# A blend whose weights move to PSUM: four convolution layers on one core

## The reference

```
x = x + L0(_gn(x))   # 1x1 conv to 288, depthwise 3x3; 8x8 circular correlation of q and k by FFT,
                     # layer norm over channels, times v, 1x1 conv back to 48
x = x + L1(_gn(x))   # 1x1 conv to 288, a mask on the FFT of 8x8 patches, depthwise 3x3, gelu gate
x = x + L2(_gn(x))   # below
x = x + L3(_gn(x))   # 1x1 conv to 192, depthwise 3x3, gelu gate, 1x1 conv, FFT mask on 8x8 patches
```

```
integ = jnp.cumsum(jnp.cumsum(x, axis=-1), axis=-2)
...
A = _grid_sample_border_bilinear(integ, off_tl)      # Bt, Ct, D: the other three corners
return (A + D - Bt - Ct) / area
```

## Time and profile before

| | |
|---|---|
| median of three executions | 36,064.37 us (35,958.09 to 36,074.78) |
| profiled execution | 36,039.24 us |
| its span, first to last instruction | 36,037.1 us |
| PE, PEld, DVE, ACT, POOL busy | 84%, 49%, 54%, 20%, 27% |
| granted TensorE clock, mean | 0.869 |

### The profile page before, as it was taken

One profiled execution on the slowest core, in us unless ns is written; L12 is line 12 of the kernel. 1 busy time (PEld: TensorE's weight loads), 2 busy tenths in 40 slices (PEclk: granted clock), 3 DMA queues, 4 the chain that ended last, 5 costly groups with the idle time before them and its releaser, 6 DMA issues. The chain is left out here.

```text
span 36037.1 us, 386987 instructions
## 1 busy us (share of the span) xinstructions
PE 30354.0 (84%) x121076; PEld 17516.0 (49%) x121076; DVE 19585.9 (54%) x30068; ACT 7293.6 (20%) x13627; POOL 9842.8 (27%) x8820
## 2 busy tenths in 40 slices
PE   3999998877779999777789989677789988777899
PEld 2664446444444446444444455445444463444566
DVE  4336774444557774444457764444467744555433
ACT  1332221121222220111222210122122211111122
POOL 0000000266640000466620000666600002777300
PEclk9999996877779996877789978777799968888999
DMA  2110001433320003333310013333300014555332
GB/s 81 33 34 14 14 15 54 97 89 85 90 64 15 14 14 88 93 89 89 88 33 14 15 33 98 85 88 87 84 18 14 14 51 104 116 115 120 89 67 64
DMA packets 756453, 2226.31 MB, mean 62 GB/s; under 512 B 217460, under 2 KB 427444, under 8 KB 621240
## 3 DMA queue, kind: packets, MB, share of 16 engines
q1 hardware_dynamic: 314304, 1181.12, 14.0%
q0 software_dynamic: 441408, 1037.60, 11.2%
HBM read 1840.72 MB, written 385.13 MB: 62 GB/s over the span
## 5 line engine op out<-in xcount | busy, mean ns | idle before, releaser
L1486 POOL DMA_INDIRECT e_got<-table,e_idx x8192 | 9470.4, 1156 | 4874.5 <-issue 2568.6
L818 PE MATMUL b_p_conv<-b_z,b_diag 96*96 96x512 f32 (+1 forms) x11616 | 5289.4, 596 | 28.8 <-DVE b_acc L937 21.1
L937 DVE SCALAR_TENSOR_TENSOR b_acc<-b_z,b_dwc,b_acc 96x512 f32<-96x512 f32 (+1 forms) x6864 | 5144.6, 750 | 243.2
L488 PE MATMUL a_p_qk<-a_wst,a_stack 128*128 128x192 f32 x12288 | 2967.1, 369 | 1013.8 <-issue 958.1
L818 PEld LDWEIGHTS b_p_conv<-b_z,b_diag 96*96 96x96 f32 (+1 forms) x11616 | 1848.9, 167 | 2481.6 <-issue 2418.2
L780 POOL DMA_DIRECT2D planes<-b_out x132 | 68.0, 515 | 10895.6 <-DVE b_out L961 10895.6
L488 PEld LDWEIGHTS a_p_qk<-a_wst,a_stack 128*128 128x128 f32 x12288 | 2168.4, 206 | 1513.3 <-issue 1401.7
L280 PE MATMUL d_p<-d_xs,d_ws 128*96 128x512 f32 x9216 | 2575.5, 424 | 215.2 <-issue 187.1
L876 ACT ACTIVATE b_ys<-b_p_in 128x304 f32<-128x304 f32 x2112 | 892.9, 423 | 7948.0 <-PE b_p_in L827 7948.0
L840 PE MATMUL b_p_z<-const,b_ym 128*96 128x128 f32 (+1 forms) x12672 | 1880.2, 288 | 601.2 <-ACT b_z L882 518.1
L840 PEld LDWEIGHTS b_p_z<-const,b_ym 128*96 128x96 f32 (+1 forms) x12672 | 1713.3, 178 | 1097.1 <-ACT b_z L882 692.1
(11 more groups left out here) (261 smaller groups left out, 40035.1 us busy)
## 6 DMA issues: line engine op xcount, KB each, us to landing
e_got<-table,e_idx POOLq DMA_INDIRECT x8192
a_stack<-in_xp SPq DMA_DIRECT2D x256, 387.0 KB
c_stack<-planes SPq DMA_DIRECT2D x256, 387.0 KB
d_stack<-planes SPq DMA_DIRECT2D x256, 387.0 KB
table<-i_acc SPq DMA_DIRECT2D x256, 384.0 KB, 2.3
b_x<-planes SPq DMA_DIRECT2D x132, 395.1 KB
b_xr<-planes POOLq DMA_DIRECT2D x132, 395.1 KB, 4.7
planes<-b_out POOLq DMA_DIRECT2D x132, 395.1 KB, 4.1
```

The lines of the kernel that those rows point to most:

```text
L488: pe.matmul(dst_, st[:, row, dx + 128 * t:dx + 128 * t + 128], wst[:, dx, 0:2 * C2], start=(dx == 0), stop=False)
L818: mm = pe.matmul(p_conv[i % 2][0:M[g], :], diag[0:M[g], base + k, 0:M[g]], z[1 - par][g][0:M[g], QROWS * q + dy:QROWS * (q + 1) + dy, dx:d ...
L937: ins = dve.scalar_tensor_tensor(out=a, in0=z[1 - par][g][0:M[g], QROWS * q + dy:QROWS * (q + 1) + dy, dx:dx + W], scalar=dwc[0:M[g], g, k ...
L1486: pool.indirect_dma_start(out=self.got[k % 4][:, t, j * REC:(j + 1) * REC], out_offset=None, in_=self.flat, in_offset=bass.IndirectOffsetO ...
```

## The change

In the joint phases with layer 0, ScalarE copies the 64 weights of a unit from SBUF into columns 384 to 447 of the bank `p_f[0]` (`weigh`), one step before the blend, and VectorE's product reads them there and not in SBUF. A semaphore `wt_copied` tells VectorE that the copy is there; `weighted`, which the product now raises in place of the first count of `halved`, tells ScalarE that the columns may be written again, and TensorE that the transforms may write the bank. With layer 3 `bank` is None, and the product reads SBUF as before.

```diff
+        spare = p_f[0][:, 4 * C2:4 * C2 + 64]
...
-                def transforms(n, k):
+                def transforms(n, k, back2):
 
                     pe.wait_ge(qk_copied, 2 * (n + 1))
+                    if boxes and back2:
+
+                        pe.wait_ge(boxes.weighted, n - 2 - 4 * S + 1)
...
+                    if boxes and back:
+
+                        boxes.weigh(act, u if 1 <= k < 8 else u - 1, (k - 1) % 8, n - 1 - 4 * S, spare)
                     if back:
                         act.wait_ge(b_ready, n)
...
-                        boxes.blend(dve, u if 2 <= k < 8 else u - 1, (k - 2) % 8, n - 2 - 4 * S)
+                        boxes.blend(dve, u if 2 <= k < 8 else u - 1, (k - 2) % 8, n - 2 - 4 * S, spare)
...
-            credit(dve, self.halved, n=4)
+            credit(dve, self.weighted)
+            credit(dve, self.halved, n=3)
...
+    def weigh(self, act, u, k, n, bank):
+
+        i, q = k // 4, k % 4
+        if q == 0:
+            act.wait_ge(self.aux_loaded[i], (self.b * self.U + u + 1) * 32)
+        act.wait_ge(self.weighted, n)
+        act.activation(bank, self.wt[i][:, 64 * q:64 * q + 64], ACT.Copy).then_inc(self.wt_copied, 1)
+
+    def blend(self, dve, u, k, n, bank):
...
+        if bank is None:
+            bank = self.wt[i][:, 64 * q:64 * q + 64]
+        else:
+            dve.wait_ge(self.wt_copied, n + 1)
         flat = got[:].rearrange("p t (k c) -> p (t k) c", c=C)
-        dve.tensor_tensor(flat, flat, self.wt[i][:, 64 * q:64 * q + 64].unsqueeze(2).broadcast_to([128, 64, C]), ALU.mult).then_inc(self.halved, 1)
+        dve.tensor_tensor(flat, flat, bank.unsqueeze(2).broadcast_to([128, 64, C]), ALU.mult).then_inc(self.weighted, 1)
+        dve.wait_ge(self.weighted, n + 1)
         for j, half in enumerate((8 * C, 4 * C, 2 * C)):
-            dve.wait_ge(self.halved, n4 + j + 1)
+            if j:
+                dve.wait_ge(self.halved, n * 3 + j)
             dve.tensor_tensor(got[:, :, 0:half], got[:, :, 0:half], got[:, :, half:2 * half], ALU.add).then_inc(self.halved, 1)
...
-                            boxes.blend(dve, pair, place, at)
+                            boxes.blend(dve, pair, place, at, None)
```

More of the change, by code:

```diff
@@ L547, in step @@
                     if front:
-                        transforms(n, k)
+                        transforms(n, k, back2)
                     if back:
@@ L561, in _ @@
                     credit(act, qk_copied, qh_copied, upper_done, n=2)
+                if boxes:
+                    boxes.weigh_credit(act)
                 act.wait_ge(weights_loaded, 16 * NLOAD * (b + 1))
@@ L1420, in __init__ @@
         (self.halved, self.used, self.v_ready, self.y_ready, self.res_ready, self.stats_done, self.turn_sem, self.cleared,
-         aux0, aux1, x0, x1, s0, s1, idx0, idx1) = semaphores(env, "e", [
+         aux0, aux1, x0, x1, s0, s1, idx0, idx1, self.weighted, self.wt_copied) = semaphores(env, "e", [
              "halved", "used", "v_ready", "y_ready", "res_ready", "stats_done", "turn", "cleared",
-             "aux_loaded0", "aux_loaded1", "x_loaded0", "x_loaded1", "stored0", "stored1", "idx_loaded0", "idx_loaded1"])
+             "aux_loaded0", "aux_loaded1", "x_loaded0", "x_loaded1", "stored0", "stored1", "idx_loaded0", "idx_loaded1", "weighted", "wt_copied"])
         self.aux_loaded, self.x_loaded, self.stored, self.idx_loaded = [aux0, aux1], [x0, x1], [s0, s1], [idx0, idx1]
@@ L1498, in clear @@
         dve.wait_ge(self.cleared, 4 * (self.b + 1))
-    def blend(self, dve, u, k, n):
+    def weigh(self, act, u, k, n, bank):
[5 more added lines that the diff above has]
+    def blend(self, dve, u, k, n, bank):
         i, q = k // 4, k % 4
@@ L1506, in blend @@
             dve.wait_ge(self.aux_loaded[i], (self.b * self.U + u + 1) * 32)
+        if bank is None:
+            bank = self.wt[i][:, 64 * q:64 * q + 64]
+        else:
+            dve.wait_ge(self.wt_copied, n + 1)
         flat = got[:].rearrange("p t (k c) -> p (t k) c", c=C)
-        dve.tensor_tensor(flat, flat, self.wt[i][:, 64 * q:64 * q + 64].unsqueeze(2).broadcast_to([128, 64, C]), ALU.mult).then_inc(self.halved, 1)
+        dve.tensor_tensor(flat, flat, bank.unsqueeze(2).broadcast_to([128, 64, C]), ALU.mult).then_inc(self.weighted, 1)
+        dve.wait_ge(self.weighted, n + 1)
         for j, half in enumerate((8 * C, 4 * C, 2 * C)):
-            dve.wait_ge(self.halved, n4 + j + 1)
+            if j:
+                dve.wait_ge(self.halved, n * 3 + j)
             dve.tensor_tensor(got[:, :, 0:half], got[:, :, 0:half], got[:, :, half:2 * half], ALU.add).then_inc(self.halved, 1)
-        dve.wait_ge(self.halved, n4 + 4)
+        dve.wait_ge(self.halved, n * 3 + 3)
         dve.tensor_tensor(self.box[:], got[:, :, 0:C], got[:, :, C:2 * C], ALU.add).then_inc(self.used, 1)
@@ L1516, in blend, with weigh_credit @@
         dve.tensor_tensor(self.val[k % 2][:, :, 1:CP], self.box[:], self.rec[i][:, 4 * q:4 * q + 4, :], ALU.mult).then_inc(self.v_ready, 1)
+    def weigh_credit(self, act):
+        if self.b == 0:
+            credit(act, self.wt_copied)
     def first_credit(self, pe):
```

## The result

The changed kernel takes 37,414.10 us (four executions, 37,232.92 to 37,454.31) against 36,034.15 us (the median of the kernel before with a fourth execution, timed beside the changed one): 1.0377 times the kernel before, 95% interval 1.0343 to 1.0410. It is slower, by 1,380 us. The profiled execution took 37,232.92 us.

The account below looks back on a forecast made before the run. Joint phases were taken to be bound by engines stuck beside GpSimd's gather stream until it pauses. Terms -260 + 207 + 512 = +459 us on the median 36,064 (profiled 36,039.24) gave 36,520 us, 1.3% slower; range 35,600 to 37,500.

Parts of the forecast that it names:

- the forecast's own case: In the joint phases stalls last longer: 36,200 to 37,100 us, chance 0.42.
- rival C: All joint-phase steps fall into a locked pattern of 32.2 us a unit: +1755 us, 37,820 us; it or near it 0.13.
- What bounds the kernel: In joint phases compute is late, not the gathers; other engines stick beside GpSimd's stream until it pauses; phases total 10,610 us.
- Item 1: VectorE's product reading its weights from PSUM keeps its 3.33 us; bounds under 8 us.
- Item 2: The product no longer holds GpSimd's gathers: 580 us of GpSimd's time, counted as -260 us, bounds 0 and -590.
- Item 3: The gather stream's pause falls from 3.5 to 1.5 us: the stuck steps cost +207 and +512 us.
- the 110 quick steps: Joint-phase steps of 17.8 us on average; counted at nothing, +540 us if a third were quick thanks to the pause.
- the stuck steps: 122 joint-phase steps: 78 with the product late by 2 to 7 us (24.1 us), 44 later still (43.8 us).
- Item 4: ScalarE's copy of 64 columns takes about 0.24 us and costs nothing; +92 us with cover gone.
- item 5: TensorE's transforms wait for the product's end, and VectorE for the weights: nothing.
- Rival A: The freed gathers pay and nobody needed the pause: faster, 35,450 or 35,750 us, chance 0.27.
- The cause that I offered: The joint loops are starved of code by the gathers' DMAs, as a taken branch breaks instruction prefetch; no size given.

Follow-up runs that it names:

- Experiments 1 and 2: experiment 1, then the changed kernel with GpSimd filling a tile twice (1.8 us each) before each joint unit's 9th gather: 0.9746, repeated 0.9747 of the kernel before.
- experiment 1: Changed kernel with VectorE's product reading SBUF again, copy, waits and semaphores kept: 1.000 of the kernel before without stalls, 1.0036 with stalls (36,103.93 us).
- experiment 3: One 1.8 us GpSimd pause per joint unit: changed kernel 0.9858 of the kernel before with stalls, 0.9951 without; the kernel before with that pause 0.9816 and 1.0162.

## Why the prediction was right and wrong

The direction was right, the size wrong: +459 us forecast, +1,380 measured, inside the range of all cases, but above the 37,100 us of the forecast's own case, and nearer to rival C (+1,755) than to the forecast. C itself isn't it: its 32.2 us are not in every step, as 78 of 381 still take under 19 us.

*What bounds the kernel* was read rightly in what matters: the stalls end when the gather stream pauses. Experiments 1 and 2 turn "seems to do the other engines a service" into a cause.

*Item 1* held: 3.33 us. *Item 2* held as to GpSimd: no issue over 2.52 us, its issues 240 us a phase shorter (2,049 to 2,066 us for 2,292 to 2,309), some 720 us in all where 580 was estimated. But the -260 us drawn from it failed. GpSimd stopping earlier means that it also starts its next stream earlier against work that isn't done. Its wait only grew, 4031.1 us in 245 places.

*Item 3* is the step that failed, by its size. Items 2 and 3 are the product's operand, priced at +459 us together; experiment 1 measures it, in another series, at +1,222. Item 3 counted the 110 quick steps at nothing, and gave no reason. Of these 110, 55 came behind a step whose product had held a gather, and 53 of those behind another quick one; the other 55 came behind a step in which GpSimd had stood. So for half of them it was a product that had broken the stream. In the changed kernel 84 products still start on time (under 11 us behind the reciprocal) beside a running stream, but their steps take 29.5 us on average, where the 110 took 17.8: the stall has moved behind the product, as at 10174 to 10211. Another 62 start on time while GpSimd stands, and take 18.4 us. It also let half the stuck steps be freed by the first add. An issue held by an add leaves a hole of 1.6 us at most, and 1.8 us per 16 gathers freed nothing in the bare streams. Its two upper bounds, 1,025 and 540 us, were nearer: with item 2 at 0 they make 1,565 us.

*Item 4* was right on the copy (0.22 us for 0.24), and nearly so on its cost: experiment 1 measures copy and waits, *item 5* with them, at 0.17 to 0.55% where stalls occur and at 0.1% or less where they don't. I said nothing, with 92 us if the cover is gone; about 90 it was.

*Rival A* was right for a chip without stalls, as far as the kernels with a pause show it (723 us), and wrong here. The Trainium skill, "SBUF — State Buffer", section Who interferes with whom, is borne out on the port: the product with one input in SBUF leaves GpSimd alone. Its sentence that TensorE and ScalarE never wait on anyone isn't, on these chips: one instruction per 1.40 us beside a dense stream of indirect gathers. That SBUF's ports are what they wait for is not shown. *The cause that I offered*, that a taken branch breaks the prefetch ("Runtime: NRT & Kernel Launch", Instruction fetch mechanics), isn't needed for the pace of the bare streams: straight code without a branch is held as a loop of 16 matmuls is. For the kernel's longer stalls, which fall on what waits for TensorE, it was not tested.

What stays open: by what way the gathers hold up the instructions of the bare streams, and TensorE's results or their signals in the kernel (the onset behind some 80 matmuls speaks for their supply, no more); why some chips don't show it, and why one chip took 35,427 us for the kernel before in one series and 35,958 in another. Nor was it settled why one short break per unit does nothing in the bare stream and much in the kernel (experiment 3), where the adds, and GpSimd's waits for a buffer, break the stream as well.

## What to carry to other kernels

A wait on an engine that isn't the bound may be what keeps the others going: before freeing it, look at what the engines around it do in the microseconds behind that wait, and count the steps that run well because of it, not only those that run badly. Beside dense indirect gathers, look for instructions that start microseconds after the TensorE result they read ("remote"), and try a deliberate break of 2 to 4 us in every 8 gathers: here it was worth 2.5% of the kernel and 5.9% of the changed one. Time such a change on more than one chip: the kernel before with the short pause was 1.6% slower on one and 1.8% faster on another.

## What the hardware showed that I had not expected

- Beside a stream of indirect DMAs, one per 1.25 to 1.4 us, TensorE and ScalarE, waiting for nobody, get one instruction per 1.40 us once some 80 matmuls have run beside it: behind 12 or 13 gathers with 192 columns, behind 29 with 512 (then a matmul of either with its weight load 2.80 us, 0.163 us alone with 192). A pause of 3.53 us after every 8 gathers removes it.
- In a kernel with waits the lateness falls on ScalarE's and VectorE's instructions that read TensorE's results (L582 late in 199 of 381 steps, by up to 39.2 us), and never on those that wait for ScalarE or VectorE (0.2 us at most).
- It occurs in some series alone, each of the two without it on a chip of its own: the same kernel took 34,077 to 34,084 us without and 35,427 to 36,034 us with it.
- In the stall TensorE's granted clock is 0.50, the lower of its levels (1.2 GHz), and 1.00 in the stages at full pace (2.4 GHz): what comes behind a stall starts slow. In the timeline above, L549 takes 1.86 us behind 8.17 us of idling, where a quick step of before has 1.05.
- A VectorE product of 3072 columns makes an issue of GpSimd take up to 4.6 us (0.95 alone) with both inputs in SBUF, and leaves it at 0.95 with one of them in PSUM; its own 3.33 us is the same.
